# Clearing an edge table in the attention stage, and starting its accumulation with the convolutions

## The reference

```python
x = x + _L0_gnn_ref(h, src, dst, W, a)            # attention
x = x + _L1_gnn_ref(h, edge_index, W, b)          # 3 convolutions
x = x + _L2_gnn_ref(h, edge_index, ...)           # gated steps, then 2 dense layers
x = x + _L3_gnn_ref(h, edge_index, edge_weight, ...)
# of L3:
msgs = edge_weight[:, None] * x[row]
agg = jax.ops.segment_sum(msgs, col, num_segments=x.shape[0])
h = (agg + x) @ W1.T + b1 + agg * x @ W2.T + b2
```

## Time and profile before

| what | us |
|---|---|
| median of three runs | 2467.09 (2464.96 to 2472.77) |
| profiled execution | 2460.7 |
| its span | 2458.9 |
| PE busy | 2203.4 (90%) |
| DVE busy | 1088.8 (44%) |
| ACT busy | 769.0 (31%) |
| POOL busy | 629.5 (26%) |
| mean granted clock of PE | 0.952 |

### The profile page before, as it was taken

How to read it: one execution, slowest core, us unless ns; L and a number is a source line. 1 busy time by engine, 2 the same in 40 slices (tenths; PEclk the granted TensorE clock), 3 DMA queues, 4 the chain that set the end, 5 groups by cost and what they waited for, 6 DMA issues and landing times.

```text
span 2458.9 us, 28185 instructions
## 1 busy us (share of the span) xinstructions
PE 2203.4 (90%) x10179; PEld 1230.9 (50%) x10180; DVE 1088.8 (44%) x3043; ACT 769.0 (31%) x1405; POOL 629.5 (26%) x425
## 2 busy tenths in 40 slices
PE   4677768889868999598999999999999999998998
PEld 3444438755544555244445554455445554454444
DVE  7499988999973456433121121222112211112202
ACT  3455547788852333222111111111111111112200
POOL 1000004300003434143444434443444344410000
PEclk9899995699998999799999999999999999999999
DMA  5444431111212111323222232223222322124583
GB/s 165 149 171 159 169 124 2 27 53 52 74 58 34 1 27 22 93 52 81 43 46 31 46 76 26 38 40 71 46 30 45 67 37 34 22 57 160 212 304 102
DMA packets 178582, 187.22 MB, mean 76 GB/s; under 512 B 101916, under 2 KB 165582, under 8 KB 174379
## 3 DMA queue, kind: packets, MB, share of 16 engines
q1 hardware_dynamic: 108474, 134.73, 16.6%
q0 software_dynamic: 56720, 1.28, 6.8%
q10 hardware_dynamic: 13260, 49.53, 5.6%
HBM read 100.83 MB, written 84.66 MB: 75 GB/s over the span
## 4 chain that ended last, share of the span: by engine, by line
PE 53%; DMA 3%; DVE 1%; issue 1%; ACT 0%; DVEq 0%; ACTq 0%
PE banks L1607 24%; PE banks L1632 21%; PE banks L1729 5%; DMA feat<-hnD 3%; PE banks L1685 1%; PE banks L1593 1%; PE banks L1694 0%; PE banks L1747 0%; DMA out_dram<-big 0%; DVE HN L1900 0%; DVE banks L1895 0%; ACT banks L1792 0%; DVE HN L1897 0%; PE banks L1744 0%; PE banks L1710 0%
## 5 line engine op out<-in xcount | busy, mean ns | idle before, releaser
L808 POOL DMA_INDIRECT WT<-lists x391 | 615.5, 1574 | 861.8 <-DMA WT<-lists 846.9
L1607 PE MATMUL banks<-big,feat 125*128 125x500 f16 (+1 forms) x3150 | 606.8, 353 | 19.4 <-DMA feat<-hnD 15.2
L1607 PEld LDWEIGHTS banks<-big,feat 125*128 125x128 f16 x3150 | 306.5, 97 | 309.9 <-DMA feat<-hnD 16.0
L1632 PE MATMUL banks<-H,U 128*128 128x500 f32 (+1 forms) x756 | 302.8, 541 | 9.4 <-issue 9.3
L1632 PE MATMUL banks<-aT,V 128*128 128x500 f32 (+1 forms) x756 | 296.4, 538 | 3.0 <-DVE HN L1900 3.0
L771 PE MATMUL banks<-ohp,ohs 128*125 128x500 f16 x628 | 164.4, 384 | 66.9 <-DVE ohp L689 66.9
L1632 PEld LDWEIGHTS banks<-aT,V 128*128 128x128 f32 x756 | 143.1, 190 | 145.1 <-issue 97.4
L1888 DVE SCALAR_TENSOR_TENSOR HN<-banks,bh,HN 128x500 f32<-128x500 f32 (+1 forms) x70 | 47.8, 682 | 378.5 <-ACT HN L1790 354.4
L1632 PEld LDWEIGHTS banks<-H,U 128*128 128x128 f32 x756 | 142.6, 191 | 139.2 <-issue 101.6
L689 DVE TENSOR_SCALAR ohp<-pairs,wcol 128x500 f16<-128x500 f16 x628 | 177.3, 351 | 0.0
L1790 ACT ACTIVATE HN<-banks,bs 128x500 f32<-128x500 f32 (+1 forms) x70 | 44.3, 633 | 381.5 <-PE banks L1632 381.5
(11 more groups left out here) (273 smaller groups left out, 2269.4 us busy)
## 6 DMA issues: line engine op xcount, KB each, us to landing
big<-WT ACTq DMA_DIRECT2D x25, 1562.5 KB, 7.5
WT<-zero SPq DMA_DIRECT2D x39, 980.0 KB, 5.1
hTD<-HN SPq DMA_DIRECT2D x40, 250.0 KB, 2.1
hnD<-stg SPq DMA_DIRECT2D x32, 250.0 KB
feat<-hnD SPq DMA_DIRECT2D x4, 2000.0 KB
H<-hTD SPq DMA_DIRECT2D x16, 500.0 KB, 4.9
work<-xhD SPq DMA_DIRECT2D x28, 250.0 KB
WT<-lists POOLq DMA_INDIRECT x391, 3.0
```

Source lines behind the costliest of these rows:

```text
L808: nc.gpsimd.indirect_dma_start(out=WT, out_offset=bass.IndirectOffsetOnAxis(ap=lists[:, 0, t - first:t - first + 1], axis=0), in_=lists[:, ...
L1607: last = nc.tensor.matmul(SUMS[s % 2][half][:, 0:wid(ch)], rows_, A[:, j, cols(ch)], start=(j == 0 and part == 0), stop=(j == T - 1 and pa ...
L1632: last = nc.tensor.matmul(PS[bank][:, 0:w], wt_[:, kt, g:g + 128], v[:, kt, 0:w], start=(n == 0), stop=(n == len(terms) - 1))
```

## The change

The 39 transfers that clear WT go from SP's queue in the count stage to SP's queue in the attention: 18 of them are issued at its start, ahead of the 49 steps, and the other 21 one in every odd step after the load of `xhD`. The tile `zero` is filled by POOL at the start of the attention, ahead of the two small fills `far` and `oneh` for which ACT and PE wait. No accumulating transfer is issued in the attention; the convolutions issue the first 70, and the recurrent stage the other 321.

```diff
-SPLIT0, SPLIT = 26, 91
+SPLIT = 70
 (prepare)
-        MADE = 15
+        MADE = 14
-                g.memset(zero[:], 0.0).then_inc(made, 1)
 (counts, sync)
-                    while z < ZF * (b + 1) // NBATCH:
-                        sp.dma_start(WT[z * LANE * ZW:(z + 1) * LANE * ZW, :].rearrange("(p a w) o -> p a (w o)", p=LANE, w=ZN),
-                                     zero[:].to_broadcast([128, ZW // ZN, ZN])).then_inc(zeros, 16)
-                        z += 1
-                sp.wait_ge(zeros, 16 * ZF)
 (attention, sync)
+                def clear(i):
+                    sp.dma_start(WT[i * (LANE * ZW):(i + 1) * (LANE * ZW), :].rearrange("(p a w) o -> p a (w o)", p=LANE, w=ZN),
+                                 zero[:].to_broadcast([128, ZW // ZN, ZN])).then_inc(zeros, 16)
+                sp.wait_ge(zero_r, 1)
+                for i in range(18):
+                    clear(i)
                 sp.wait_ge(mx_r, T)
                 for s, (ch, g) in enumerate(steps):
                     ... (fetch(s + 2), residual(0))
+                    if s % 2 and 18 + s // 2 < ZF:
+                        clear(18 + s // 2)
...
                 sp.wait_ge(xh_out, 16 * SC)
+                sp.wait_ge(zeros, 16 * ZF)
 (attention, gpsimd)
+                nc.gpsimd.memset(zero[:], 0.0).then_inc(zero_r, 1)
                 nc.gpsimd.memset(far[:], BIG).then_inc(made, 1)
                 nc.gpsimd.memset(oneh[:], 1.0).then_inc(made, 1)
-                scatter(nc, pool, scat_sems, lists0, scatD, WT, 0, SPLIT0)
 (convolutions, gpsimd)
-                scatter(nc, pool, scat_sems, lists1, scatD, WT, SPLIT0, SPLIT)
+                scatter(nc, pool, scat_sems, lists1, scatD, WT, 0, SPLIT)
```

More of the change, by code:

```diff
@@ L115, in gnn_kernel @@
                     dump=sb("dump", [128, 1]),
-                    zero=sb("zero", [128, 1, ZN]),
                     scol=col[:, 0, :],
@@ L165, in prepare @@
         sb = pieces(big)
-        (ecol, wcol, wp, rank, visits, scol, trow, ident, identh, pairs, nodes, first, dump, zero) = (edges[n] for n in (
-            "ecol", "wcol", "wp", "rank", "visits", "scol", "trow", "ident", "identh", "pairs", "nodes", "first", "dump", "zero"))
+        (ecol, wcol, wp, rank, visits, scol, trow, ident, identh, pairs, nodes, first, dump) = (edges[n] for n in (
+            "ecol", "wcol", "wp", "rank", "visits", "scol", "trow", "ident", "identh", "pairs", "nodes", "first", "dump"))
         ei = sb("ei", [128, 2, EG, LANE], i32)
@@ L624, in sb @@
             return c.enter_context(nc.sbuf_tensor(name, shape, dt))
-        comb, sib, keyc, wc, wp, rank, wcol, visits, pairs, nodes, first, dump, zero = (edges[n] for n in (
-            "comb", "sib", "keyc", "wc", "wp", "rank", "wcol", "visits", "pairs", "nodes", "first", "dump", "zero"))
+        comb, sib, keyc, wc, wp, rank, wcol, visits, pairs, nodes, first, dump = (edges[n] for n in (
+            "comb", "sib", "keyc", "wc", "wp", "rank", "wcol", "visits", "pairs", "nodes", "first", "dump"))
         ohp = sb("ohp", [128, 2, SPAN, WC], f16)
@@ L635, in counts @@
         scat = wcol[:].rearrange("p a r -> p (a r)").bitcast(i32)[:, 0:2 * TILES].rearrange("p (k t) -> p k t", k=2)
-        names = ("oh_made", "win_r", "win_out", "x_made", "x_prod", "x_added", "gap_r", "eq_r", "eq_used", "outs", "chain", "zeros", "dve_did")
-        (oh_made, win_r, win_out, x_made, x_prod, x_added, gap_r, eq_r, eq_used, outs, chain, zeros, dve_did) = (sem("w_" + n) for n in names)
+        names = ("oh_made", "win_r", "win_out", "x_made", "x_prod", "x_added", "gap_r", "eq_r", "eq_used", "outs", "chain", "dve_did")
+        (oh_made, win_r, win_out, x_made, x_prod, x_added, gap_r, eq_r, eq_used, outs, chain, dve_did) = (sem("w_" + n) for n in names)
         d_in = [sem(f"w_d{i}") for i in range(RD)]
@@ L664, in _ @@
             def _(sp):
-                z = 0
                 for b in range(NBATCH):
@@ L803, in scatter @@
     got, added = sems
-    stage = (0, SPLIT0, SPLIT).index(first)
+    stage = (0, SPLIT).index(first)
     pool.dma_start(lists[:], scatD[:, :, first:end]).then_inc(got, 16)
@@ L817, in sb @@
             return c.enter_context(nc.sbuf_tensor(name, shape, dt))
-        lists0 = sb("lists0", [128, 2, SPLIT0], i32)
+        zero = sb("zero0", [128, 1, ZN])
         z = sb("z", [P, 2 * NQ, CH])
@@ L840, in attention @@
         names = ("made", "loaded", "neg_r", "mx_r", "deg_r", "al_r", "l_r", "e_r", "p_r", "tp_r", "ev_r",
-                 "mm_r", "hT_r", "o_r", "y_r", "exp_r", "x_in", "x1_r", "x1_out", "n_r", "xh_r", "xh_out", "chain")
+                 "mm_r", "hT_r", "o_r", "y_r", "exp_r", "x_in", "x1_r", "x1_out", "n_r", "xh_r", "xh_out", "chain", "zero_r", "zeros")
         (made, loaded, neg_r, mx_r, deg_r, al_r, l_r, e_r, p_r, tp_r, ev_r,
-         mm_r, hT_r, o_r, y_r, exp_r, x_in, x1_r, x1_out, n_r, xh_r, xh_out, chain) = (sem("a0_" + n) for n in names)
+         mm_r, hT_r, o_r, y_r, exp_r, x_in, x1_r, x1_out, n_r, xh_r, xh_out, chain, zero_r, zeros) = (sem("a0_" + n) for n in names)
         xh_in = [sem(f"a0_xh{i}") for i in range(RX)]
@@ L1154, in sb @@
             return c.enter_context(nc.sbuf_tensor(name, shape, dt))
-        lists1 = sb("lists1", [128, 2, SPLIT - SPLIT0], i32)
+        lists1 = sb("lists1", [128, 2, SPLIT], i32)
         words = feat[:].rearrange("p t a d -> p (t a d)")
```

## The result

The changed kernel takes 2473.32 us (median of 20 runs, 2464.56 to 2486.48); the kernel before, beside it, 2467.16 us (20 runs, 2463.06 to 2473.00). The ratio is 1.0029, 95% interval 1.0016 to 1.0042: about 7 us slower (the two medians lie 6.2 apart), where 12.0 were forecast. The runs of the changed kernel are spread over 22 us, those of the kernel before over 10. The profiled execution took 2473.85 us (span 2470.9), against 2460.7 (span 2458.9).

What follows compares the result with a forecast made beforehand. DVE bounds the count stage and attention, PE the recurrent stage; what decides is when POOL's transfer chain ends against ACT's wait. 0.5 + 9.1 + 2.4 = +12.0 us on 2460.7 gives 2472.7, as median 2479.1; range 2466 to 2489.

Steps and rivals of the forecast that it cites:

- The count stage: Count stage: losing 39 clearing transfers gains 0 us, as DVE sets the pace; rival of a speed-up there, chance 0.04 with other gains.
- The fill of zero: Start of the attention: POOL's fill of `zero` now precedes `oneh`, which ACT's first activation awaits; +0.5 us.
- The scatters that leave the attention: Attention: 26 accumulating transfers leave, 0 us, as DVE's passes did not feel them; at most 3.8 us gain if POOL were to blame.
- The clears in the attention: Attention: 39 clears arrive, 18 at its start and 21 in odd steps, all hidden; 0 us.
- the 10.9 us of cover: Attention's steps: time from an xhD load's issue to the product reading it, against at most 5.1 us for a clear ahead.
- The rival of colliding clears: Attention: xhD loads queue behind clears beyond their cover, perhaps 5 to 10 us longer, about 2486; chance 0.08.
- The convolutions: Convolutions: 70 accumulating transfers instead of 65, ending at 998 us with 24 us of cover; 0 us.
- The tail: End of the recurrent stage: 21 more transfers, last landing at 2262.4, 9.1 us after ACT must start; +9.1 us.
- The thin load: Chain's end, 2228 to 2242: the long load of x2D delays the accumulating transfers by 9.2 us.
- the first burst: Chain's end, 2204 to 2212: loads for the dense layers fill the DMA engines and cost the chain 6.2 us.
- The clock: Dense layers: after PE stands still for about 10 us, its granted clock is at the lower level; +2.4 us.
- That the chain ends in time: End of the recurrent stage: last transfer lands by 2253.3, only the 0.5 stays, 2467.6; rival, chance 0.20.

Runs made afterwards that it cites:

- POOL's clears: Changed kernel with the 21 clears of the attention's steps issued from POOL's queue instead of SP's: 2488.31 us, ratio 1.0073 to the kernel before.
- the split alone: Kernel before with only the accumulating transfers redivided to 0, 70 and 321, clears still in the count stage: 2477.06 us, ratio 1.0046.
- the split at 60: Changed kernel with 60 accumulating transfers in the convolutions and 331 in the recurrent stage: 2526.27 us, ratio 1.0228.
- the covered kernels: Changed kernel with its last 21 accumulating transfers left out, ratio 1.0007, or with ACT's wait and five first table-row loads moved later, ratio 1.0024.
- the split with late loads: Kernel before with transfers divided 0, 70, 321, ACT's wait at the first table-row load, five first loads at dense steps 4 to 7: 2468.12 us, ratio 1.0002.

## Why the prediction was right, point by point

**The count stage, 0: right.** The comparisons take 255.3 us instead of 255.5. The sign that I had named, the same mean of line 689, would have misled: the recorded length was 496 ns instead of 353 in one profile and 353 in the next, at the same pace. The 0.282 us of the prediction is neither that length nor the pace, which is 50 / 123 = 0.41 us; it is busy time by count, in which neighbouring records overlap. The conclusion stands all the same.

**The fill of zero, +0.5: right.** It stands ahead of ACT's first activation. From the last comparison to the last maximum it is 102.8 us in both profiles of the kernel before, 103.6 and 103.3 in the two of the changed one.

**The scatters that leave the attention, 0: right.** The 25 passes keep their 3.416 us with POOL idle, and their spacing its 3.57. But the reason given, that the equal lengths speak against a lock, looked at one side only. Two rows of the trace of before:

```profile
399.57 3.42 DVE L1050 CUSTOM_DVE_ANT_0 work<-trow,z 125x3125 f32<-125x3125 f32 x1
402.63 1.78 POOL L808 DMA_INDIRECT WT<-lists  x1 [1.79 <-DMA WT<-lists]
```

POOL's issue begins 0.36 us before this pass ends and is over 1.42 us after it. So are 25 of the 26, in both profiles of the kernel before: they begin 0.24 to 0.54 us ahead of the end of a pass and end 1.41 to 1.45 us after it, last 1.65 to 1.97 us where 1.55 is usual, and so follow each other at the passes' 3.57 us instead of 3.3. The page of the Trainium skill, *SBUF — State Buffer*, section "SBUF: two separate sides", lets DVE and GpSimd lock each other out, and the one that starts first keeps the ports; the traces agree, with POOL as the one that waits. No part of the 3.8 us came back since DVE had never waited.

**The clears in the attention, 0: wrong, they cost 2 to 3 us in the profiles.** The 18 at the start went as worked out, 47 us for 50 forecast. Two rows follow, the stretch 380 to 430 of the changed kernel (PE, PEld, DVE, ACT, POOL; clock; DMA share; GB/s), and the 21 clears of the steps with their times to landing:

```profile
380.00:430.00 50.00, 45.22 (x342) 44.48 (x342) 47.98 (x29) 40.65 (x15) 0.00 (x0) 0.50 1.05 315
...
L896 SPq DMA_DIRECT2D WT<-zero x21: 518/519/1589, 485.0 to 702.4; - x21
...
DMA to landing us min/median/max: 6.8/7.8/11.2
```

Two terms of this step failed. One is the 5.1 us as the most that a clear can take: that was its time in a stage where little else moved. Among the fetches and stores of the attention it is 7.8 us, up to 11.2. The other is the 10.9 us of cover, read off a single early load. Late in the stage the steps are shorter; two rows of the trace of before, the load of a step and the first product that reads it:

```profile
658.30 0.25 SPq L885 DMA_DIRECT2D work<-xhD  x1
...
666.52 0.87 PE L1013 MATMUL banks<-work 125*128 125x375 f32 x2
```

That is 8.2 us, and the shortest is 8.1. All the waits of PE for xhD fall into this late part, between 641 and 716 us: 4 or 5 of them, 3.4 to 6.0 us together in the seven executions with the 18 and 21 clears on SP's queue. The steps took 264.0 us on average in these seven, 261.7 in the five with none among the fetches. The ranges overlap (259.9 to 266.3 and 259.7 to 262.9), and within each sort the executions with a granted clock of 0.95 over the steps are the short ones, those with 0.94 the long ones, so a part of the difference between single executions is not the clears'. The rival of colliding clears had the mechanism, with a price that was too high, 5 to 10 us.

**The convolutions, 0: right.** The last of the 70 is issued at 1005.0, 28 us ahead of the next stage. That is later than the 1000 named as a sign, since the stage began later; the 70 took 250.0 us from first to last, and 250.5 were forecast.

**The tail, +9.1: right in its mechanism and its place, too large on average.** In the changed kernel's first profile it is 1.1 us, and its terms can be set beside rows one by one. The first 300 transfers, "as before" at 1136.0 us, took 1132.8, which is 3.2 less. The 21 were to take 21 x 3.36 plus 21.4 for other loads, 92.0 us; they took 84.5, which is 7.5 less. The thin load with the burst ahead of it cost 11.1 us (10.22 + 7.49 - 6.6), for 12.2 forecast. But the first burst, at 2214 to 2222, cost 2.3 us for 6.2 forecast (a spacing of 5.6), though the engines were 0.64 and 1.00 busy there, and the loads of dense(3) and dense(4) cost nothing, for 3: the first of them left at 2260.5, after the last transfer was issued. So a transfer does not always lose as long as the engines are full. Against these stands the last landing, which I took as 3.3 us after the issue. The trace gives it as:

```profile
L800 POOL DMA_INDIRECT WT<-lists x1: 1549/1549/1549, 2259.1 to 2259.1; - x1
DMA to landing us min/median/max: 6.1/6.1/6.1
```

That is 2.8 us more, and ACT starts 0.07 us after it: ACT is not slow, the landing is late. In all, 9.1 - 3.2 - 7.5 + 2.8 = 1.2, the 1.1 measured. The late landing belongs to the last of the 391 transfers: 5.9 and 6.5 us in the two profiles of before, where nobody waited for it, 6.1 to 8.9 in the others, and 3.0 for the 370th where that is the last. The forecast could have read it.

Over the executions the same terms vary: 84.5 to 88.9 us for the 21 in nine of them, 1129 to 1149 for the first 300 of a split at 70, 6.1 to 8.1 from the last issue to ACT in all six where ACT waited for it at this place. So the tail's loss at the narrow products was 1.1, 4.8, 8.4 and 8.9 us in four executions with the same 21, and 15.9 in the one with POOL's clears. The forecast had one value where there is a distribution, and took an upper-middle one: 9.1 lies near the 8.9 of the split alone, and in the one execution that it was set against the agreement is gone.

**The clock, +2.4: right where the tail is long.** In the split alone the loss grows by 3.1 us from the first narrow to the first table product, with the split at 60 by 2.1, in the changed kernel's second profile by 1.6, and in its first, where PE stood for 0.97 us, by 0.1. The granted clock over 2270 to 2275 of the split alone is 0.50, the lower level, and 0.94 over the next 10 us.

**The sum.** Forecast 12.0 over the profiled execution; measured 7 over the median (4 to 10 by the interval). The profiled execution of the changed kernel came out at 2473.85, beside 2472.7 forecast, but by other terms: 1.1 of tail and 10.8 ahead of it, of which the repeated profiles show that about 4 us in prepare and up to 3 in the attention come and go with any kernel. That this one profile agrees with the sum is luck.

**The signs.** ACT held by the landing, the spacing near 10 us and the last issue near 2260 came. The loads of xhD that nobody waits for did not. And one sign of being wrong did come, an attention longer than 364.5 us, which I had counted from 371 to 735: from POOL's first fill to its load of the next stage's lists it is 373.2 us in the changed kernel's first profile where it was 367.0. But it is 367.5 in its second, and 370.1 in the second profile of the kernel before, so a single profile cannot be judged by this sign.

**The rivals.** That the chain ends in time is refuted by the wait itself, in every execution with 21 or more and the wait where it was; the spacings beside the load of x2D were 10.22 and 7.49 us. It came near, though: with the measured terms above only 1.1 us were missing in one profile. The spacings show that the rule of the Trainium skill, *DMA: Bandwidth & Descriptors*, section "Queues, rings and completion order", that an engine takes turns between queues packet by packet, doesn't make a small accumulating transfer cheap beside the load of x2D; beside the first burst it got through with 2.3 us lost. The count stage gave nothing back.

What stays open: how the 7 us divide. By the medians the covered kernels keep 2 to 6 of them, which leaves 1 to 5 for the tail, but the intervals allow more or less of either. Nor do the parts add up: the split alone costs 11 us and the clears come on top of it, yet the changed kernel with both costs 7. The intervals overlap (1.0028 to 1.0064 and 1.0016 to 1.0042), so this may be scatter. Open as well why the same 300 transfers take 1129 us in one execution and 1149 in another, and why the 391st lands 3 us later than the others. Its 144 packets are over 2.9 us after the issue, like those of the rest; only what tells of the landing comes late.

## What to carry to other kernels

A serial chain beside a busy engine has no cost until its end passes the place where it is awaited, and from there each of its steps adds its full length: ask where the wait stands, and put it at the first instruction that reads the result, with the first such read as late as its consumer allows. Here that takes a loss of 11 us to none, by moving one wait and five loads. And profile the same kernel twice before a difference of a few microseconds in a stage is explained.

## What the runs showed of the hardware

- The duration recorded for a DVE comparison (median) was 353 ns in one profile of the changed kernel and 496 in another, at an unchanged rate of 124 in 50 us; the split with late loads has 478 with the clears beside it, the kernel before 353. It says nothing on the pace.
- While DVE makes its passes of 3.416 us over 3125 values, an accumulating transfer's issue on POOL ends 1.41 to 1.45 us after the end of a pass, though it begins 0.24 to 0.54 us before it: 25 of 26 in both profiles of the kernel before. DVE loses nothing by it.
- Filling one table by 39 clears of 1.0 MB: back to back 2.6 us each (315 GB/s, DMA share 1.05), 5.1 us to land in a stage with little else, 7.8 us among the fetches of the attention.
- A second queue was no help: with the clears on POOL's queue PE waited 7.4 us for the fetches, with both on SP's queue 3.4 to 6.0.
- Issuing can take as long as moving: 18 clears held SP's queue for 47 us, and behind 32 of them three fetches of 250 KB took 8.72 us to issue instead of 1.06.
- A dependent accumulating transfer takes 3.3 us in quiet, with little scatter; beside the load of x2D two in a row take 8.7 to 10.7 and 5.0 to 9.2 us, in all eleven traces where the chain reaches it. The last of the 391 lands 5.9 to 8.9 us after its issue in every trace that has it, and ACT resumes 0.07 us after the landing.
